# Moving two small steps in the queues of ScalarE and GpSimd in a causal-attention kernel

## The reference

```python
q, k, v = (x @ w.T + b).reshape(B, S, 16, 64)   # for each of the three
scores = einsum('bqhd,bkhd->bhqk', q, k) / 8     # causal: -inf above the diagonal
probs = softmax(scores)
attn = einsum('bhqk,bkhd->bqhd', probs, v).reshape(B, S, D)
out = attn @ wo.T + bo
```

## Time and profile before

| | us |
|---|---|
| median of 3 runs | 2400.26 |
| the runs | 2400.26, 2402.63, 2395.5 |
| profiled execution, its own time | 2394.96 |
| its span (first to last instruction) | 2392.7 |
| mean granted TensorE clock | 0.982 of full |
| busy in the span: TensorE, ScalarE, VectorE, GpSimd | 2272.9, 1746.1, 1689.8, 1657.7 |

### The profile page before, as it was taken

One profiled execution on the slowest core, in us unless ns is written; L12 is line 12 of the kernel. 1 busy time (PEld: TensorE's weight loads), 2 busy tenths in 40 slices (PEclk: granted clock), 3 DMA queues, 4 the chain that ended last, 5 costly groups with the idle time before them and its releaser, 6 DMA issues. The chain is left out here.

```text
span 2392.7 us, 70688 instructions
## 1 busy us (share of the span) xinstructions
PE 2272.9 (95%) x28666; PEld 1450.0 (61%) x28666; DVE 1689.8 (71%) x4148; ACT 1746.1 (73%) x2380; POOL 1657.7 (69%) x1291
## 2 busy tenths in 40 slices
PE   6999999999999998899999999999999689999996
PEld 4566667675757665557575757575766445445453
DVE  8487777777777766566666666666676846777777
ACT  6477777877788766677777777777788746666665
POOL 3588888888888876678888888888898832222221
PEclk9999999999999999999999999999999889999998
DMA  9699999999999999999999999999999985656662
GB/s 246 123 187 203 204 213 204 199 197 204 205 202 205 208 200 202 206 200 190 183 191 182 188 182 182 191 180 188 179 199 199 228 169 151 169 153 172 150 168 80
DMA packets 1380627, 447.43 MB, mean 187 GB/s; under 512 B 1325104, under 2 KB 1358272, under 8 KB 1380304
## 3 DMA queue, kind: packets, MB, share of 16 engines
q1 hardware_dynamic: 1380304, 442.91, 99.2%
HBM read 67.95 MB, written 41.94 MB: 46 GB/s over the span
## 5 line engine op out<-in xcount | busy, mean ns | idle before, releaser
L1049 POOL TENSOR_TENSOR hl<-probs,hl 128x1024 f16<-128x1024 f32 x544 | 1171.4, 2161 | 155.9 <-ACT hl L901 155.3
L894 ACT ACTIVATE probs<-s_ps,exp_bias 128x1024 f32<-128x1024 f32 (+7 forms) x768 | 633.7, 854 | 295.4 <-DVE exp_bias L727 292.2
L722 DVE TENSOR_REDUCE neg_max<-s_ps 128x1 f32<-128x1024 f32 (+7 forms) x768 | 676.4, 905 | 149.6 <-PE s_ps L524 146.6
L901 ACT ACTIVATE hl<-probs 128x1024 f16<-128x1024 f32 x544 | 575.0, 1057 | 84.8 <-DMA pt<-hl 68.6
L547 PE MATMUL o_ps<-v,pt 128*128 128x65 f16 x4352 | 432.8, 193 | 45.5 <-DMA pt<-hl 40.1
L547 PEld LDWEIGHTS o_ps<-v,pt 128*128 128x128 f16 x4352 | 401.4, 97 | 73.8 <-DMA pt<-hl 28.7
L548 PE MATMUL o_ps<-v,pt 128*128 128x65 f16 x4352 | 433.0, 194 | 0.0
L549 PE MATMUL o_ps<-v,pt 128*128 128x65 f16 x4352 | 431.7, 192 | 0.0
L524 PE MATMUL s_ps<-nat 64*128 64x512 f16 (+3 forms) x3840 | 410.2, 352 | 21.6 <-ACT probs L894 18.6
L548 PEld LDWEIGHTS o_ps<-v,pt 128*128 128x128 f16 x4352 | 400.7, 97 | 19.3
L549 PEld LDWEIGHTS o_ps<-v,pt 128*128 128x128 f16 x4352 | 401.2, 98 | 0.0
(11 more groups left out here) (185 smaller groups left out, 3613.2 us busy)
## 6 DMA issues: line engine op xcount, KB each, us to landing
w_raw<-in_w_pairs SPq DMA_DIRECT2D x48, 576.0 KB, 4.8
o_scratch<-o_hl SPq DMA_DIRECT2D x64, 256.0 KB, 3.3
out<-result SPq DMA_DIRECT2D x31, 512.0 KB, 3.3
x_in<-in_x SPq DMA_DIRECT2D x27, 512.0 KB, 4.9
pt<-hl SPq DMA_TRANSPOSE x544, 5.3
xn_scratch<-xn SPq DMA_DIRECT2D x16, 512.0 KB, 4.7
xn<-in_x SPq DMA_DIRECT2D x11, 512.0 KB, 4.1
x_in_c<-in_x SPq DMA_DIRECT2D x10, 512.0 KB, 4.2
```

The lines of the kernel that those rows point to most:

```text
L722: nc.vector.tensor_reduce(neg_max[:, step.round, acc, h:h + 1], s_ps[(n + h) % S_RING][:, first:end], AX_X, ALU.max, negate=True).then_inc ...
L894: last = nc.scalar.activation(probs_of(n)[:, cols], s_ps[n % S_RING][:, cols], ACT.Exp, bias=exp_bias[:, step.round, acc, h:h + 1], scale= ...
L901: nc.scalar.activation(hl_of(n, 0), probs_of(n), ACT.Copy).then_inc(p_hi_done, 1)
L1049: nc.gpsimd.tensor_tensor(hl_of(n, 1), probs_of(n), hl_of(n, 0), ALU.subtract).then_inc(p_lo_done, 1)
```

## The change

In each step that opens a round, GpSimd's `long_rows` moves from the head of the step to a place behind head 0's `probs_low` and behind `unit_low`. Where finished rows are split, `rows_low` moves behind `unit_low` and head 1's `probs_low`, and ScalarE's `rows_high` moves behind `unit_high` and head 1's exponentials. No instruction is added or removed, and no wait is changed.

```diff
 # ScalarE, body(p, kind), for i in range(NSTEP):
                     if step:
                         exponentials(*step, 0)
                     if steps_of(p)[i].opens:
                         chunk_factors(p, steps_of(p)[i].round)
-                    if i == half_done(p) or i == 0 and p > 0:
-                        rows_high(2 * p + (0 if i else -1))
                     for u in units_ending(kind, i - 1):
                         unit_high(units_of(p), u)
                     if step:
                         exponentials(*step, 1)
+                    if i == half_done(p) or i == 0 and p > 0:
+                        rows_high(2 * p + (0 if i else -1))
 # GpSimd, body(p, kind), for i in range(NSTEP):
                     step = step_of(p, i, kind)
+                    if step:
+                        probs_low(*step, 0)
+                    for u in units_ending(kind, i - 1):
+                        unit_low(units_of(p), u)
                     if steps_of(p)[i].opens and (p or i):
                         long_rows(*((p, steps_of(p)[i].round - 1) if i else (p - 1, N_ROUND - 1)))
                     if step:
-                        probs_low(*step, 0)
+                        probs_low(*step, 1)
                     if i == half_done(p) or i == 0 and p > 0:
                         rows_low(2 * p + (0 if i else -1))
-                    for u in units_ending(kind, i - 1):
-                        unit_low(units_of(p), u)
-                    if step:
-                        probs_low(*step, 1)
```

## The result

| | before | after |
|---|---|---|
| median, us (22 runs each) | 2399.78 | 2402.24 |
| lowest to highest | 2393.26 to 2402.99 | 2398.41 to 2407.49 |
| span of the profiled execution | 2392.7 | 2404.2 |

The ratio after to before is 1.0013, with a 95% interval of 1.0007 to 1.0019. The two profiled executions differ by far more, 11.5 us. Before's lies at the low end of its runs and after's near the high end of its own, so their difference isn't the effect of the change.

The account below looks back on a forecast made before the run. TensorE was taken as the bound, idle only 0.6 of 680 us in six steady pairs. Ten stalls of 0.43 us gave 4.3 us, all other terms 0: 2400.26 + 4.3 = 2404.5 us, range 2396 to 2414.

Parts of the forecast that it names:

- The removed wait, worth nothing: GpSimd before the first low part: an equal or longer wait for the high part replaces `inv_long`'s; 0.35 us gained, worth 0.
- Rival 2: TensorE's tile and exponential waits: earlier low parts shorten them, 28 us faster (2372), or 10 us (2390); chance 9%.
- the reading by occupancy: Six steady pairs: GpSimd, 83% busy against TensorE's 67% weight loading, would be the bound and its idle worth recovering.
- `rows_high` waits, and TensorE with it: Middle steps: `rows_high` waits at least 0.46 us for `long_rows`; TensorE's `scores` stall 0.43 us in ten pairs, 4.3 us slower.
- Ten pairs were named: Pairs 1, 2, 4, 5 and 8 to 13, where `scores` follows ScalarE's exponential by only 0.14 to 0.18 us.
- Rival 1: Middle steps: ScalarE isn't late or `scores` absorbs it; 0 to 1.5 us faster, 2400; chance 17%.
- `rows_low` late, VectorE waits 1.7 us, cost nothing: VectorE's short rows of the next round wait 1.7 us for `rows_low`; margins of 4 and 2.4 us, cost 0.
- Rival 3: VectorE holds GpSimd at `long_rows`' new place, 1.43 us instead of 0.40; ten stalls of 1.46 us, 14.6 slower, 2415; chance 12%.
- I cost the earlier low parts and `unit_low` at 0: GpSimd in steps opening a round: SyncE's queue covers any gain; without that cover, 10 us at the very most.
- contention for the port in one direction only: GpSimd's `long_rows`: VectorE operations with two SBUF inputs, such as `split_weight`, could hold it, 1.43 us against 0.40.
- nothing gives a stall back: TensorE, taken as the bound: each of ten stalls of 0.43 us adds fully to the time, 4.3 us.
- The forecast median, 2404.5: Whole kernel: median before of 2400.26 us plus 4.3 us of stalls.

Follow-up runs that it names:

- experiment 7: Kernel before, with each `probs_low` doing half its width from the third pair on: 2396.16 us, ratio 0.9984.
- experiment 1: Changed kernel with `long_rows` put back at the head of the step, the splits staying late: 2399.86 us, ratio 1.0001 to before.
- experiment 2: Changed kernel with `long_rows` behind head 0's `probs_low` but ahead of `unit_low`: 2401.37 us, ratio 1.0011 to before.
- experiment 4: Changed kernel with `unit_low` done twice in the middle step, ahead of `long_rows`: 2420.22 us, ratio 1.0087 to before.
- Experiment 5: Changed kernel with `long_rows` back at the head of the step and `unit_low` done twice in the middle step: 2400.27 us, ratio 1.0010 to before.
- experiment 6: Changed kernel with `long_rows` put back at the head in step 15 alone: 2401.27 us, ratio 1.0007 to before.
- experiment 3: Kernel before with only `long_rows` moved, behind head 0's `probs_low`, the splits where they were: 2431.98 us, ratio 1.0137.

## Why the prediction was right, and what it missed

**The removed wait, worth nothing: right.** The wait for `inv_long` has turned into a wait for the high part, 3.60 us in pair 10 against the 3.6 worked out. The sum of both kinds grew by 13 us, which I haven't traced further. I said the high part's wait would grow by about 151; it grew by 153.5. TensorE's waits for tiles stand at 40.3 us against 40.1, and experiment 7 bounds the value of a faster GpSimd from above. Rival 2 (faster, through earlier low parts) is out, and with it the reading by occupancy.

**`rows_high` waits, and TensorE with it: right in place, number and size.** Ten pairs were named, and in these ten the series steps. The working said at least 0.46 us of wait on ScalarE and 0.43 us on TensorE. Measured are 0.60 us on ScalarE in pair 10 (it came to `rows_high` earlier than the latest time that I had bounded) and 0.42 to 0.47 us on TensorE in nine of the ten. Pair 9 has 0.18, and its rows before tell why:

```profile
1230.60 1.06 ACT L919 ACTIVATE o_hl<-o_rows 128x1024 f16<-128x1024 f32 x1 [0.41 <-issue]
...
1234.33 1.10 ACT L894 ACTIVATE probs<-s_ps,exp_bias 128x1024 f32<-128x1024 f32 x1
1235.57 1.48 PE L524 MATMUL s_ps<-nat 64*128 64x256 f16 x18 [0.17 <-POOL v L1054]
```

Before, `rows_high` was already held up here, 0.41 us (the profile doesn't say by what; pair 10's wasn't), and TensorE already waited 0.17 us. Its `scores` start 0.14 us after the exponential's end at 1235.43, the usual hand-over, so it was the exponential that it waited for, whatever the label says. After, ScalarE waits 0.59 us and TensorE 0.35 us, as in pair 10. The new stall is as long as elsewhere, and takes the place of the old one. In pair 4 TensorE's 0.47 us before had no such wait of `rows_high` behind them, and grew to 0.93. The sum is 4.1 us against 4.3. Experiments 1 and 2 take the stalls away by moving `long_rows` alone, and 4 lengthens them by 1.18 us, with 1.19 us of work put ahead of it, where 5 has the same work and none of the stalls. Rival 1 (hidden) is out.

**`rows_low` late, VectorE waits 1.7 us, cost nothing: right.** The wait is 1.83 us in pair 10. Experiment 5 makes it 3.0 us in each steady pair without a stall in the middle steps.

**Rival 3, a blocked `long_rows`: out.** `long_rows` takes 0.40 us at its new place in pair 10.

**What the prediction missed.** The term that was wrong is "I cost the earlier low parts and `unit_low` at 0". It asked only what an earlier low part could gain, and the list of places was drawn up by who waits for `rows_high`. It left out what the low part meets once it starts first. In step 15 of pair 1 that is `norm_apply`, in step 15 of pair 4 `xn_low`, and they cost 2.6 us in these two places. I had weighed contention for the port in one direction only (VectorE holding GpSimd), and the Trainium skill, "SBUF — State Buffer", Who interferes with whom, gives both directions: whichever issues first holds the shared pair, and a VectorE `tensor_scalar` is among the operations that can contend for it. The traces agree: `norm_apply` takes 0.88 us before, 0.89 in experiment 6, and 2.62 after.

**Why the total came out near although a term was missing.** In part by luck. 4.1 + 2.6 = 6.7 us stand in the series, and the timed difference is 3.1 (1.7 to 4.6). So at least 2 us of the stalls don't show in the time, where the prediction said that nothing gives a stall back. That error and the missing term have opposite signs. The parts don't say where the time comes back: 2.6 us alone times as 2.6 (0.5 to 4.6, experiment 2), and 4.1 us alone as 1.7 (-1.0 to 4.6, experiment 6); both intervals hold the whole sum. Experiments 3 and 4 time close to the whole of their stalls. (The forecast median, 2404.5, also stood on three runs before with a median of 2400.26; over 22 it is 2399.78.) One place where the two traces differ the other way is pair 3, where TensorE waits for a tile. Its stretch before and then after (same columns as in the earlier trace rows):

```profile
520.00:525.00 5.00, 2.06 (x32) 1.79 (x34) 0.57 (x3) 3.75 (x4) 4.10 (x4) 0.81 1.27 180
525.00:530.00 5.00, 5.00 (x72) 3.91 (x69) 3.41 (x12) 2.32 (x4) 3.33 (x2) 0.85 1.03 200
```

```profile
520.00:525.00 5.00, 3.27 (x81) 3.04 (x80) 2.26 (x5) 4.59 (x5) 5.00 (x4) 1.00 1.11 171
525.00:530.00 5.00, 5.00 (x87) 4.45 (x82) 4.41 (x17) 4.46 (x6) 4.50 (x3) 1.00 1.13 207
```

Before, TensorE waits 3.1 us for the tile here and then runs below the full clock. After, it comes 2 us later, waits 1.7 us and keeps the clock. The series falls by 3 us, from +2.04 to -0.94, and climbs back to +0.19 by step 3 of pair 4, after ScalarE has waited 4.7 us for a transposed tile.

Lateness alone doesn't explain the fall. The series falls by 3 us in experiment 6, which came late (+2.45 to -0.63), but also in 7, which came on time (-0.04 to -2.92). It doesn't in experiment 1 (+0.07 to +0.15), and not in 2 (+1.92 to +2.29), 3 (+4.87 to +6.15) or 4 (+5.02 to +4.75), which came as late or later; in 5 it falls by 1.1. What goes with the fall is a short wait. In the three traces that have it TensorE waits 1.4 to 1.8 us here and keeps the clock. In before and the other five it waits 2.0 to 3.5 us, and 3.4 us or more at half the clock follow. Why the wait was short isn't shown, and each of these is one execution.

Nor is the rest of the 11.5 us between the two profiled spans settled. In the trace after, it arises in the turn of pairs 6 and 7 (+3.1 us) and in the last pair (+2), where TensorE waits for transfers. In that turn the series rises in all seven experiments too, by 1.9 to 5.5 us, also in those that time like before or faster. It was before's profiled execution that was quick there, and the rise isn't a mark of the change.

**What the sizes of experiments 3 and 4 show.** I expected less of both. The difference is 2.6 us for pairs 2 and 5 in each, pair 14's stall in experiment 3, and the clock behind the longer stalls: five spells in experiment 3 and one in 4.

## What to carry to other kernels

When an operation is moved behind others on an engine, time its consumer on the next engine and that one's consumer in turn: here 0.04 us of slack at `scores` decided that a wait of half a microsecond on ScalarE went on to TensorE almost whole. Then look at what the operation that takes its place starts beside, in both directions. And before paying for a shorter wait on the second busiest engine, ask with one cheap run what that engine's time is worth: half of GpSimd's low-part work left out bought 3.8 us of 2400.

## What the hardware showed that I had not expected

- A stall of TensorE of 2.1 us, in work that otherwise had no gap, was followed in five of eleven places by 3.4 us at 1.2 instead of 2.4 GHz, 1.6 us of further delay each (experiment 3). Stalls of 1.6 us were followed by it in one of ten (experiment 4), stalls of 0.4 us in none. What decides among the eleven stays open.
- VectorE's `norm_apply`, 128x1024 in f32 with SBUF on both sides, took 2.62 us beside a GpSimd low part that was under way, and 0.88 us when it came first. The low part took 3.12 us and 2.58 us in the two cases instead of its usual 2.14. VectorE's `xn_low`, of the same width with two inputs, took 3.15 us against 1.42.
- Of VectorE's `norm_apply` and `xn_low`, the trace after has three operations 1.7 us longer than before, and two others 1.2 and 1.8 us shorter, though VectorE's own order wasn't touched. Only the two in step 15 show in the series.
